# A graph network on one core: message bias laid into PSUM by ACT, and the next group's x turned between the gates

## What is computed

```python
h = relu(layernorm(x))
x = x + L0(h, adj)                       # below
h = relu(layernorm(x))
x = x + adj @ (h @ weight) + bias        # the second layer

def L0(x, mask):
    c1 = relu(bn1(conv1(x)));  x_conv = relu(bn2(conv2(c1, 17 taps)) + x)
    s = x @ w_se.T + b_se                # 3 columns
    dist = |s_n|^2 + |s_m|^2 - 2 s_n.s_m
    A = exp(-dist) * mask
    msg = relu(x @ w_msg.T + b_msg)      # 128 columns
    x_nmp = A @ msg
    gi = [x_conv, x_nmp] @ w_ih.T + b_ih;  gh = x @ w_hh.T + b_hh     # GRU cell
    r = sigmoid(gi_r + gh_r);  z = sigmoid(gi_z + gh_z)
    return (1 - z) * tanh(gi_n + r * gh_n) + z * x
```

## Time and profile before

| | us |
|---|---|
| runs (three) | 378.32, 378.87, 379.08; median 378.87 |
| the profiled execution | 378.42 |
| its span | 376.5 |
| PE busy in the span | 341.2 (91%), 2212 matmuls |
| PEld busy | 311.8 (83%) |
| DVE busy | 286.4 (76%) |
| ACT busy | 208.7 (55%) |
| POOL busy | 174.1 (46%) |

### The profile page before, as it was taken

One profiled execution on the slowest core, in us unless ns is written; L12 is line 12 of the kernel. 1 busy time (PEld: TensorE's weight loads), 2 busy tenths in 40 slices (PEclk: granted clock), 3 DMA queues, 4 the chain that ended last, 5 costly groups with the idle time before them and its releaser, 6 DMA issues.

```text
span 376.5 us, 6337 instructions
## 1 busy us (share of the span) xinstructions
PE 341.2 (91%) x2212; PEld 311.8 (83%) x2212; DVE 286.4 (76%) x737; ACT 208.7 (55%) x403; POOL 174.1 (46%) x140
## 2 busy tenths in 40 slices
PE   5758776979999999999999999999999999989864
PEld 5757776769998899889988999889988998989663
DVE  4596688797878997797879887889767987653572
ACT  1545733576854686548744785468645835262242
POOL 7763247212890179224951298118911594072022
PEclk9886889998999999999999999999999999999998
DMA  7700020000220013000310031001100010000001
GB/s 256 275 3 0 0 66 20 0 1 2 86 83 2 1 58 113 0 0 30 105 36 1 2 112 57 0 2 65 49 1 2 0 57 1 3 28 30 0 0 57
DMA packets 7951, 15.10 MB, mean 40 GB/s; under 512 B 1008, under 2 KB 1648, under 8 KB 7792
## 3 DMA queue, kind: packets, MB, share of 16 engines
q1 hardware_dynamic: 7632, 14.56, 11.1%
q10 hardware_dynamic: 288, 0.14, 0.1%
HBM read 10.50 MB, written 4.19 MB: 39 GB/s over the span
## 4 chain that ended last, share of the span: by engine, by line
issue 40%; POOL 28%; PE 13%; DVE 11%; ACT 5%; DMA 1%; SPq 0%; POOLq 0%; DVEq 0%; ACTq 0%
POOL rs L1161 3%; POOL ac L838 3%; POOL px L842 3%; POOL base L1213 3%; POOL x_ring L1203 3%; POOL base L1215 3%; POOL px L832 3%; POOL px L840 2%; POOL px L835 2%; POOL base L1219 2%; POOL rs L1156 2%; ACT hn L601 1%; DMA x_ring<-x_in 1%; DVE cx_lo L931 1%; DVE st L855 1%
## 5 line engine op out<-in xcount | busy, mean ns | idle before, releaser
L1161 POOL TENSOR_TENSOR rs<-ve,neg_half 128x4 f32<-128x4 f32 x16 | 16.1, 1009 | 103.8 <-DVE ve L972 103.8
L280 PE MATMUL pP<-cx_hi,conv_hi 128*128 128x256 f32 x176 | 54.4, 309 | 5.6 <-DVE cx_lo L931 5.6
L281 PE MATMUL pP<-cx_lo,conv_hi 128*128 128x256 f32 x176 | 52.0, 296 | 0.0
L282 PE MATMUL pP<-cx_hi,conv_lo 128*128 128x256 f32 x176 | 52.0, 296 | 0.0
L280 PE MATMUL pQ<-cx_hi,conv_hi 128*128 128x256 f32 x144 | 46.0, 319 | 2.7 <-issue 2.2
L281 PE MATMUL pQ<-cx_lo,conv_hi 128*128 128x256 f32 x144 | 43.2, 300 | 0.0
L282 PE MATMUL pQ<-cx_hi,conv_lo 128*128 128x256 f32 x144 | 43.1, 299 | 0.0
L1156 POOL TENSOR_TENSOR rs<-ve,neg_half 128x8 f32<-128x8 f32 (+1 forms) x9 | 14.9, 1656 | 56.5 <-DVE ve L862 56.5
L280 PEld LDWEIGHTS pP<-cx_hi,conv_hi 128*128 128x128 f32 x176 | 34.4, 195 | 6.0 <-DVE conv_lo L936 3.5
L931 DVE TENSOR_TENSOR cx_lo<-px,cx_hi 128x576 fp32r<-128x576 f32 x32 | 35.0, 1116 | 0.6 <-ACT cx_hi L590 0.6
L282 PEld LDWEIGHTS pP<-cx_hi,conv_lo 128*128 128x128 f32 x176 | 34.3, 195 | 0.0
(11 more groups left out here) (246 smaller groups left out, 1022.3 us busy)
## 6 DMA issues: line engine op xcount, KB each, us to landing
x_ring<-x_in SPq DMA_DIRECT2D x16, 256.0 KB, 2.6
adj_ring<-adj_in SPq DMA_DIRECT2D x16, 256.0 KB, 3.3
out<-x_ring SPq DMA_DIRECT2D x15, 256.0 KB, 2.0
work<-conv_in SPq DMA_DIRECT2D x1, 1088.0 KB, 7.5
x_ring<-gate_in SPq DMA_DIRECT2D x1, 576.0 KB, 7.9
out<-x_ring SPq DMA_DIRECT2D x2, 128.0 KB, 1.7
work<-bias_in SPq DMA_DIRECT2D x1, 132.0 KB, 7.4
early<-early_in SPq DMA_DIRECT2D x1, 129.5 KB, 2.9
```

The lines of the kernel that those rows point to most:

```text
L280: pe.matmul(acc, w_hi, m_hi, start=start, stop=False)
L281: pe.matmul(acc, w_hi, m_lo, start=False, stop=False)
L282: return pe.matmul(acc, w_lo, m_hi, start=False, stop=stop)
L1161: pool.tensor_tensor(rs2[g % 2][:], ve2[g % 2][:], neg_half[:, 0:GG], ALU.pow).then_inc(rs2_set, 1)
```

## The change

1. The bias row is now in SBUF on all 128 partitions (`bias`, 128 x 131), and a new ACT function `place_bias(g)` copies it four times into pNR. TensorE's `messages` loses the two matmuls with ones per group and adds its products onto what lies in the bank; it waits for `bias_placed`. So that the products add, both banks are written once by a matmul in the opening (two 128 x 512 matmuls with the identity in place of seven of `keep_clock`). `place_bias(a)` stands in the gates of the step before, between `reset_gate(q)` and `update_gate(q)`; `place_bias(b)` stands in the step behind ACT's `messages(a)` and waits for it.
2. For groups 6, 8, 10, 12 and 14 the turn of x (`x_turn`), ACT's `hidden` and DVE's `hidden_lo` move from the head of a step into the gates of the step before: on TensorE between `gates_h(q)` and `gates_n(q)`, on ACT between `hidden_gate(q)` and `reset_gate(q)`, on DVE between `blend_end(p)` and `normalise1`. In step 1 they stay at the head.
3. The rounding of the bias on ACT, its remainder on DVE and the memset of the ones on POOL go away.

```diff
--- before.py
+++ after.py
...
@@ -342,19 +339,11 @@
...
 
             def messages(g):
-                if g == 0:
-                    pe.wait_ge(bias_split, 1)
-                    pe.wait_ge(rows_zero, 1)
                 have(pe, hT_set, g + 1)
-                if g % 2 == 0 and g > 2:
-                    have(pe, ghn_set, g - 2)
-                    have(pe, tr_set, g - 2)
-                else:
-                    have(pe, msg_set, g)
-                for i in range(2):
-                    pe.matmul(ms[:, 2 * i:2 * i + 2, 0:MP], ones_r[:], bias_r[:], start=True, stop=False)
-                    for j in range(2 * i, 2 * i + 2):
-                        last = pe.matmul(ms[:, j, 0:MS], graph(half(hT, g), j), w_ms, start=False, stop=j % 2 == 1)
+                pe.wait_ge(bias_placed, g + 1)
+                for j in range(GG):
+                    last = pe.matmul(ms[:, j, 0:MS], graph(half(hT, g), j), w_ms, start=False, stop=True,
+                                     skip_group_check=True)
                 last.then_inc(ms_done, 1)
 
@@ -452,7 +441,11 @@
...
             def opening():
                 pe.wait_ge(ident_set, 1)
-                keep_clock(17)
+                for bank in (pN, pR):
+                    last = pe.matmul(bank.rearrange("p (g n) -> p g n", g=GG), ident[:],
+                                     ident[:].unsqueeze(1).to_broadcast([128, GG, N]), start=True, stop=True)
+                last.then_inc(ms_marked, 1)
+                keep_clock(10)
                 x_turn(0)
                 x_turn(1)
@@ -506,7 +499,7 @@
...
                 a, b, p, q, pp, qq = 2 * t + 2, 2 * t + 3, 2 * t, 2 * t + 1, 2 * t - 2, 2 * t - 1
                 front, middle = t + 1 < NS, t < NS
-                if front:
+                if t == 1:
                     x_turn(a)
                 o_turn(pp)
@@ -563,6 +556,8 @@
...
                     if not front:
                         o_turn(p)
+                    if t + 2 < NS:
+                        x_turn(a + 2)
                     gates_n(q)
                     gates_c(q)
@@ -621,6 +616,18 @@
...
                                bias=bn_b[:, 0:1], scale=bn_a[:, 0:1]).then_inc(c1_set, 1)
 
+            def place_bias(g):
+                if g == 0:
+                    act.wait_ge(bias_loaded, 16)
+                    act.wait_ge(ms_marked, 1)
+                elif g % 2 == 0 and g > 2:
+                    act.wait_ge(ghn_set, g - 2)
+                    act.wait_ge(tr_set, g - 2)
+                else:
+                    act.wait_ge(msg_set, g)
+                act.activation(ms[:, :, 0:MS], bias[:].unsqueeze(1).to_broadcast([128, GG, MS]), ACT.Copy)\
+                   .then_inc(bias_placed, 1)
+
             def messages(g):
                 have(act, s_set, g + 1)
...
@@ -706,7 +713,11 @@
...
                     first(5)
                 hidden_gate(q)
+                if 0 < t < NS - 2:
+                    hidden(p + 4)
                 reset_gate(q)
+                if t + 2 < NS:
+                    place_bias(p + 4)
                 update_gate(q)
 
@@ -718,17 +729,18 @@
...
                 hidden(0)
                 hidden(1)
-                act.wait_ge(bias_loaded, 16)
-                act.activation(bias_r[:], bias_raw, ACT.Copy).then_inc(bias_rounded, 1)
+                place_bias(0)
                 conv1_out(0)
                 round_w(0)
...
                 split_hi(0, 0)
                 messages(0)
+                place_bias(1)
                 round_w(1)
                 split_hi(0, 1)
                 left_rows(0)
                 messages(1)
+                place_bias(2)
                 round_w(2)
                 decay(0)
@@ -746,6 +758,7 @@
...
                 split_hi(0, 4)
                 messages(2)
+                place_bias(3)
                 sums_hi(1)
                 act.wait_ge(gate_loaded, 16)
@@ -766,12 +779,13 @@
...
                 a, b, pp, qq = 2 * t + 2, 2 * t + 3, 2 * t - 2, 2 * t - 1
                 front, middle = t + 1 < NS, t < NS
-                if front:
+                if t == 1:
                     hidden(a)
                 candidate(qq)
...
                     conv1_out(a)
                     messages(a)
+                    place_bias(b)
                     hidden(b)
                 second(pp)
...
@@ -1019,6 +1033,8 @@
...
                     shift1([4, 5])
                 blend_end(p)
+                if 0 < t < NS - 2:
+                    hidden_lo(p + 4)
                 if t + 3 < NS:
                     normalise1([p + 6, p + 7])
@@ -1032,9 +1048,6 @@
...
                 hidden_lo(0)
                 hidden_lo(1)
-                dve.wait_ge(bias_rounded, 1)
-                dve.tensor_tensor(bias_r[32:64, :], bias_raw[32:64], bias_r[32:64, :].bitcast(F32), ALU.subtract)\
-                   .then_inc(bias_split, 1)
                 split_w(0)
                 split_lo(0, 0)
@@ -1282,9 +1294,7 @@
...
     vec = np.stack([f["bn1_g"], f["bn1_b"], f["bn1_m"], f["bn1_v"], f["bn2_g"], f["bn2_b"], f["bn2_m"], f["bn2_v"],
                     *f["b_ih"].reshape(3, D), *f["b_hh"].reshape(3, D)], axis=1)
-    row = np.concatenate([f["b_msg"], f["b_se"], np.zeros(1, np.float32)])
-    bias = np.zeros((128, 2 * MP), np.float32)
-    bias[0] = bias[32] = np.tile(row, 2)
+    bias = np.broadcast_to(np.concatenate([f["b_msg"], f["b_se"]]), (128, MS))
     by_phase = (QN, 2, 2)
     x = p["x"].reshape(B, *by_phase, D).transpose(3, 2, 1, 0, 4)
```

More of the change, by code:

```diff
@@ L23 @@
 MS = D + S
-MP = MS + 1
 SR = 4 * (S + 1)
@@ L65, in gnn_kernel @@
         gate_lo = sb("gate_lo", [128, 9 * D], F32R)
-        bias_raw = work[:, NW * D:NW * D + 2 * MP]
-        bias_r = sb("bias_r", [128, 2 * MP], F32R)
-        ones_r = sb("ones_r", [128, 128], F32R)
+        bias = sb("bias", [128, MS])
         late = sb("late", [128, 2 * D])
@@ L147, in gnn_kernel @@
             sem, ("ident_zero", "ident_set", "pads_set", "ones_set", "rows_zero"))
-        early_rounded, early_split, gate_rounded, gate_split, bias_rounded, bias_split = map(
-            sem, ("early_rounded", "early_split", "gate_rounded", "gate_split", "bias_rounded", "bias_split"))
+        early_rounded, early_split, gate_rounded, gate_split, ms_marked, bias_placed = map(
+            sem, ("early_rounded", "early_split", "gate_rounded", "gate_split", "ms_marked", "bias_placed"))
         wsum_set, w_rounded, w_split = map(sem, ("wsum_set", "w_rounded", "w_split"))
@@ L244, in _ @@
             sp.dma_start(conv[:, 0:TAPS * D], conv_in).then_inc(conv_loaded, 16)
-            sp.dma_start(bias_raw, bias_in).then_inc(bias_loaded, 16)
+            sp.dma_start(bias[:], bias_in).then_inc(bias_loaded, 16)
             load_x(2)
@@ L633, in left_rows @@
                 if g == 0:
-                    act.wait_ge(rows_zero, 2)
+                    act.wait_ge(rows_zero, 1)
                 act.activation(left[0:GG * SR, :], rows_bank(g)[0:GG * SR, 0:N], ACT.Copy).then_inc(left_set, 1)
@@ L912, in right_rows @@
                 if g == 0:
-                    dve.wait_ge(rows_zero, 3)
+                    dve.wait_ge(rows_zero, 2)
                 dve.tensor_tensor(right[0:GG * SR], rows_bank(g)[GG * SR:2 * GG * SR, 0:N].unsqueeze(1)
@@ L1143, in _ @@
                                pattern=[[-1, 128]], channel_multiplier=1).then_inc(ident_set, 1)
-            pool.memset(ones_r[:].bitcast(F32), 1.0).then_inc(rows_zero, 1)
             pool.memset(px[:, X32:X23 + 1, :, QP - 1:QP], 0.0)
```

## The result

| us | before | after |
|---|---|---|
| median of 17 runs each, taken side by side | 378.32 | 379.63 |
| profiled execution | 378.42 | 380.14 |
| its span | 376.5 | 378.3 |
| PE busy in the span | 341.2 (91%) | 338.3 (89%) |
| DVE busy | 286.4 (76%) | 283.4 (75%) |

The ratio after to before is 1.0046, 95% interval 1.0028 to 1.0063: slower, by 1.1 to 2.4 us. TensorE shows 42 matmuls fewer (2170 against 2212) and is busy 2.9 us less, ACT 10 us more, and the end is later.

What follows compares the result with a forecast made beforehand. TensorE was taken as saturated, but twice a step held by DVE's queue, then ACT. Opening -0.35, step 1 +0.1, steps 2 to 5 +1.6, step 6 -0.1 make +1.25 on 378.42: 379.7 profiled, 380.1 as median; range 378.1 to 382.6.

Steps and rivals of the forecast that it cites:

- conv1(a) is held by the residual, not by h_lo: First convolution of group a: 0.51 late, released by the later-ending residual, so it still waits after the change.
- +1.0 - 0.98: DVE, steps 2 to 5: L942 1.0 later through moved hidden_lo, 0.98 given back by removing h_lo(a) at the head.
- hidden_lo on DVE is not free: DVE in the gates, ahead of normalise1: 0.68 waiting plus 0.61 pitch, L942 1.0 to 1.1 us late.
- place_bias(b) adds 0.66 to the chain: ACT between messages(a) and hidden(b): hidden(b), then h_lo(b) and conv1(b), 0.66 later; bounds 0.5 and 0.85.
- The ones matmuls are worth 0.28, once per step: TensorE messages: 0.28 saved per group; messages(b)'s counts, messages(a)'s is spent waiting for h_lo(b).
- Per step +0.40: Steps 2 to 5: +1.0 - 0.98 + 0.66 - 0.28 us each, +1.6 for four; bounds +0.1 to +0.8 per step.
- Step 6, -0.1: Step whose preceding gates lack normalise1: 0.5 - 0.98 + 0.66 - 0.28 = -0.1 us.
- Step 1, +0.1: Step 1, turn still at head: 0.17 - 0.5 + 0.66 - 0.28, taken as +0.1 us; bounds -0.5 and +0.8.
- Opening, -0.35: Opening: shorter messages(2) before x_turn(3), where DVE idled 1.26 before h_lo(3); -0.35 us, bounds -0.9 and +0.6.
- The naive gain: Rival, whole kernel: early turn removes stalls and TensorE gets all it is spared, 7.3 over five steps, 371 us; chance 0.07.
- The case in which DVE's queue does not hold up: Rival, h_lo(p+4) before normalise1: hT ready when DVE comes, -0.1 per step, -0.75 in all, 378.1 us; chance 0.12.
- The clock rival: Rival, steps: conv1 stalls of 1.4 and 0.5 lower the granted clock, 1.4 us each, four times 5.5, 385.6 us; chance 0.08.

Runs made afterwards that it cites:

- e2: Kernel before with only x_turn, hidden and hidden_lo moved into the gates, bias still by ones matmuls; 378.23 us, ratio 1.0014.
- e3: Kernel after with hidden_lo(p+4) behind normalise1 on DVE instead of ahead of it; 376.57 us, ratio 0.9975.
- e4: Kernel after with place_bias(b) behind hidden(b) on ACT instead of ahead of it; 375.88 us, ratio 0.9945.
- e6: Kernel before with the ones matmuls taken out and nothing in their place, so no bias; 376.48 us, ratio 0.9954.
- e1: Kernel after with x_turn, hidden and hidden_lo back at the step's head, only the bias part left; 380.65 us, ratio 1.0081.
- e7: e5 with hidden(b) ahead of messages(a) on ACT; 370.51 us, ratio 0.9788.
- e10: e7 with eight more unread matmuls in the ending and eight behind the last second layer but one; 370.47 us, ratio 0.9790.
- e5: Kernel after with the edits of e3 and e4 together; 373.63 us, ratio 0.9867.
- e8: e1 with place_bias(b) behind hidden(b) on ACT; 377.20 us, ratio 0.9958.

## Why the prediction was right

Forecast: 1.25 us longer, 380.1, with 0.57 on slower. The ratio says 1.1 to 2.4 us longer and the after kernel's median is 379.63. The steady steps came by the steps of the sum; the parts around them did not, and that the total came so close is in part luck.

**conv1(a) is held by the residual, not by h_lo.** Forecast: the turn's move does not shorten the step's head, the stall stays near 0.5. Measured: 0.40 idle (0.36 before), again "issue", and 165.87 stands 0.09 behind the end of the residual (165.09 + 0.69). e2 puts the whole turn part at 0 to 0.02 us a step, where the sum had +1.0 - 0.98.

**hidden_lo on DVE is not free.** Forecast: 0.68 of waiting, blend_start(q) at 163.1. Measured: 0.61 and 163.16. e3 takes the wait away and gets 0.57 us a step. The turn among TensorE's gates cost a little less than the 0.50 taken: from its start to o_turn it is 162.99 - 158.36 = 4.63, where the same gates without it took 162.48 - 158.27 = 4.21, so 0.42.

**place_bias(b) adds 0.66 to the chain.** Measured 0.68 (1.17 - 0.49), and e4 gets 0.69 a step. The pitch behind it was 0.55 where 0.51 was taken, its duration 0.61.

**The ones matmuls are worth 0.28, once per step.** Measured 0.25, and e6, without any bias, gains 0.24 a step and not 0.5. conv1(b)'s wait of 1.24 lies in the forecast's 1.2 to 1.5. One reading in the sum for conv1(b) was off: 0.43 is what four transposes take with fp32 work behind them, but a split product follows there, and with one behind them they took 0.36 (162.91 to 163.27), so conv1(b) was 0.54 late before the change and not 0.47. No term of the total hangs on it.

**Per step +0.40.** Measured +0.45, +0.45, +0.45 (steps 2 to 5); e1's part is 0.43. The upper end of the range, 382.6, follows from no bound of the sum (378.87 + 4.6 is 383.5); the median lies well below either.

**Step 6, -0.1.** Measured 40.40 - 40.50 = -0.10, with no idle time before conv1(a). e2 shows it from the other side, 39.97.

**Step 1, +0.1: mis-sized.** The distance from conv1(4) to conv1(6) grew by 0.38, nearly as in the other steps, against the -0.07 that the sum has behind conv1(4) (+0.1 less the 0.17 ahead of it). The term was the bias matmuls at the low clock, taken as 0.28 / 0.54 = 0.5. These are the messages of group 4 before and after.

```profile
85.37 0.42 PE L355 MATMUL pNR<-bias_r,ones_r 128*128 128x264 f32 x1
...
87.17 0.60 PE L330 MATMUL pF<-ident,hn 128*128 128x128 f32 x4
```

```profile
84.64 1.91 PE L345 MATMUL pNR<-early,hT 128*128 128x131 f32 x8
86.39 0.60 PE L327 MATMUL pF<-ident,hn 128*128 128x128 f32 x4
```

1.80 against 1.75: the cut brought 0.05. Before, 1.14 us of full-speed work took 1.80, so only about 0.66 of it can have run at half speed and the rest already at 2.4 GHz. After, 0.89 of work took 1.75, all at half speed: the work saved was the part that had run at the full clock. The granted clock in stretches of half a us agrees: it was back at 1.00 at about 86.8 us before (0.76 over 86.5 to 87) and at about 86.4 after (0.62 over 86 to 86.5), that is inside these messages before and at their end after. With 0.05 in place of 0.5 the term is +0.5, and the forecast of the stretch from conv1(4) to step 7 becomes 1.43 + 0.45 = 1.9, against 2.05 measured. e6 bears the size out: without any bias the distance from conv1(4) to conv1(6) fell by 0.27 (41.04 from 41.31), which the 0.25 of messages(5) nearly fills. Still, e7 and e10 differ by 1.26 us in that distance with the same code there, so the 0.45 belongs to these executions.

**Opening, -0.35: its mechanism was seen, its size was not shown.** The idle 1.26 us of DVE before h_lo(3) is gone:

```profile
42.74 0.69 DVE L896 SCALAR_TENSOR_TENSOR h_lo<-pF,h_hi 128x512 fp32r<-128x512 f32 x1
```

conv1(4) came 0.72 us earlier in the profiled execution. But over the profiles of kernels with the same opening as the one after (e1, e3, e4, e5 among them) conv1(4) came at 82.86, 82.03, 83.96 and 84.44, so a single one can't show 0.35. e8 says what laying the bias by ACT costs there: with the same opening as the kernel after it has the ratio of e6, 0.9958 and 0.9954, and the same 246.98 us from conv1(4) to step 7, so an opening with the bias laid by ACT and one without a bias differ by no more than the two intervals leave open, about 1.2 us. The timed runs bound opening and tail together: 1.06 to 2.38 us by the ratio, less the 2.05 between them, is -1.0 to +0.3. The forecast's -0.35 lies in it, and so does zero.

**The tail, +0.47, was in no term.** Second layer of the last group but one, before and then after:

```profile
366.25 1.16 PE L450 MATMUL pZ<-late,work 128*128 128x128 f32 x8 [0.69 <-ACT work L655]
```

```profile
368.04 2.08 PE L439 MATMUL pZ<-late,work 128*128 128x128 f32 x8 [0.69 <-ACT work L662]
```

The instructions and the waits ahead are the same; the granted clock had fallen about 4 us sooner (1.00 over 366 to 370 us before, 0.53 after; by finer stretches at about 370.1 and 366.3). The change does nothing there that would explain it, and why the clock fell sooner stays open. The same product took 1.16 us in the profiles of e3, e4 and e7 and 2.07 in those of e1, e2, e5, e6 and e8, all with the same tail, and the tails of these eight lie between 43.99 and 45.12 us, so 0.47 is within what one execution differs from another. The timed runs do differ in one number: the granted clock averaged over the whole execution is 0.959 in the middle of the 17 runs after, and 0.964 to 0.968 in the three series before. They do not say where in the kernel the low clock lay. In the two profiles opening and tail, -0.72 and +0.47, cancel in part. The sum has 1.43 where 2.05 was measured between them, so that the medians lie 1.31 apart, within 0.1 of the forecast's 1.25, is luck; the steps are not.

**The rivals.** The naive gain (371) fails at once: TensorE at 91% of the span and 98% of the steady part got 0.5 us less to do per step, and e6 banks half of it even when nothing is put on ACT. The rule of the Trainium skill, "Perfetto Trace Analysis", Identifying the Most-Contended Engine, to optimise the engine with the highest occupancy first, names TensorE, and read as taking work off that engine it is borne out here by half: 0.5 us of work less brought 0.24 a step (e6). What brought more was to shorten TensorE's waits: e3, e4 and e7 take nothing from it, only reorder ACT and DVE, which are busy 58% and 75%, and bring 0.57, 0.69 and 0.36 us a step. The case in which DVE's queue does not hold up did not come: DVE waited 0.61. The clock rival fell: a wait of 1.24 with another of 0.40 in each 41 us left the granted clock at 1.00 from 87 us to the tail. What the Trainium skill, "TensorE: Matmul & The Clock Gate", A second HAM failure mode: psum-queue depth-cycling, tells of, short idles between groups of matmuls that make the clock oscillate, did not come in these steps.

## What to carry to other kernels

Work taken from a nearly saturated engine counts only up to the next instruction that waits for someone else; find that instruction, follow its chain back, and ask whether the replacement lands inside the chain. Here it did, between msg(a) and hidden(b), and two lines further down the same queue it cost nothing (e4, e8). Before adding an operation to an engine with spare time, look for a gap that ends with a wait, and put a moved read behind work that is already ready, not ahead of it (e3).

## What the runs showed of the hardware that was not expected

ACT writes 128 x 524 floats from SBUF into two PSUM banks in 612 to 620 ns, in all sixteen, and the next operation of its queue starts 0.55 us behind its start; that is close to its SBUF to SBUF copy of 128 x 512 (0.63 us, the next 0.53 behind it).

A stretch at 1.2 GHz is not a fixed tax. In step 1 the distance from conv1(4) to conv1(6) was 41.65 us in e10 and 40.39 in e7, with the same code there, with the granted clock at 0.63 over 87 to 90 us in the one and 0.93 in the other. A saving of matmul work that falls into such a stretch can go nearly unseen, as that of messages(4) did: 0.25 of full-speed work brought 0.05. In the kernel before, the granted clock fell within an idle time of 2.56 us (it is 0.83 over 83 to 83.5 us), though TensorE had been busy for all of the 5 us from 76 to 81.

Up to conv1(4) the profiles of kernels with the same opening differ by 2.4 us (82.03 in e3, 84.44 in e5), while in the steady steps of any one of them the period varies by 0.02 to 0.04. A difference below 1 us is read from the period, not from the span.
